# Attention inside a fused block on one core: two running-sum buffers, three low-query buffers, maxima dealt one step earlier, and two more steps per unit summed by GpSimd

## The reference

```
h      = layernorm(x) * (1 + ca) + sa
c_kv   = h @ W_kv_down
k, v   = c_kv @ W_k_up, c_kv @ W_v_up        # 16 heads of 32
q      = h @ W_q
scores = (q k^T + q_rope k_rope^T) / sqrt(64)   # q_rope, k_rope shared by all heads
w      = softmax(causal(scores))
x      = x + ga * ((w v) @ W_o)
h      = layernorm(x) * (1 + cb) + sb
x      = x + gb * (sigmoid(xr W_r^T) * (relu(xk W_k^T)^2 W_v^T))   # xr, xk: token-shifted mixes of h
```

## Time and profile before

| | |
|---|---|
| median of 3 runs | 3613.83 us (3613.76 to 3614.35) |
| the profiled execution's own time | 3614.24 us |
| its span, first to last instruction | 3612.5 us |
| PE, DVE, ACT, POOL busy over the span | 97%, 71%, 50%, 74% |
| attention stage | 472.6 to 2841.7 us |
| unit 8, from its first score matmul to the next unit's | 1667.66 to 1813.99 us, 146.33 us |
| mean granted TensorE clock | 0.992 |

### The profile page before, as it was taken

One profiled execution on the slowest core, in us unless ns is written; L12 is line 12 of the kernel. 1 busy time (PEld: TensorE's weight loads), 2 busy tenths in 40 slices (PEclk: granted clock), 3 DMA queues, 4 the chain that ended last, 5 costly groups with the idle time before them and its releaser, 6 DMA issues. The chain is left out here.

```text
span 3612.5 us, 54216 instructions
## 1 busy us (share of the span) xinstructions
PE 3494.5 (97%) x19552; PEld 2416.0 (67%) x19552; DVE 2562.3 (71%) x5329; ACT 1820.9 (50%) x3455; POOL 2673.0 (74%) x1194
## 2 busy tenths in 40 slices
PE   8999989999999999999999999999999699999999
PEld 4777756666666666666666666666665488888887
DVE  6676677777777777777777777777775366666665
ACT  2333335555555555565555555555555344444443
POOL 2333349889898898898988989889889566666665
PEclk9999999999999999999999999999999899999999
DMA  5778773463534635536346354463551111212120
GB/s 203 272 271 306 254 175 76 104 145 74 134 86 108 138 82 115 120 92 138 83 100 149 76 124 98 97 141 79 114 132 60 62 59 70 70 70 71 70 70 36
DMA packets 232756, 426.58 MB, mean 118 GB/s; under 512 B 25380, under 2 KB 26916, under 8 KB 232488
## 3 DMA queue, kind: packets, MB, share of 16 engines
q1 hardware_dynamic: 232424, 423.10, 43.5%
q10 hardware_dynamic: 64, 0.02, 0.0%
HBM read 300.86 MB, written 121.65 MB: 117 GB/s over the span
## 5 line engine op out<-in xcount | busy, mean ns | idle before, releaser
L1035 ACT ACTIVATE att_probs<-att_ps_s 128x512 f32<-128x512 f32 (+3 forms) x2560 | 1309.3, 536 | 914.6 <-PE att_ps_s L1195 810.6
L1134 POOL TENSOR_TENSOR att_sum_g<-att_sum_g,att_probs 128x2048 f32<-128x2048 f32 (+3 forms) x400 | 1625.2, 4063 | 46.4 <-ACT att_probs L1035 1.7
L1071 DVE TENSOR_REDUCE att_piece_max<-att_ps_m 128x1 f32<-128x512 f32 x1520 | 963.3, 684 | 303.4 <-PE att_ps_m L1178 300.8
L1194 PE MATMUL att_ps_s<-att_q_a,att_k_a 128*128 128x512 f32 (+3 forms) x2560 | 952.3, 376 | 18.8 <-DMA att_q_b<-att_neg_max 9.0
L1195 PE MATMUL att_ps_s<-att_q_b,att_k_b 65*128 65x512 f32 (+3 forms) x2560 | 932.5, 368 | 0.0
L1074 DVE CUSTOM_DVE_ANT_0 att_ps_m<-att_ps_m,mask_qk 128x128 f32<-128x128 f32 x1008 | 477.7, 513 | 259.7 <-PE att_ps_m L1178 246.2
L1178 PE MATMUL att_ps_m<-att_k_a,att_q_a 128*128 128x512 f32 (+3 forms) x1808 | 643.6, 381 | 1.5 <-DVE att_piece_max L1071 0.9
L1194 PEld LDWEIGHTS att_ps_s<-att_q_a,att_k_a 128*128 128x128 f32 x2560 | 485.7, 190 | 158.3 <-issue 54.0
L1201 PE MATMUL att_ps_o<-att_probs,att_v 128*32 128x512 f32 (+3 forms) x5120 | 547.1, 536 | 4.2 <-POOL att_probs L1115 4.2
L1195 PEld LDWEIGHTS att_ps_s<-att_q_b,att_k_b 65*128 65x128 f32 x2560 | 484.5, 189 | 62.6
L1178 PEld LDWEIGHTS att_ps_m<-att_k_a,att_q_a 128*128 128x128 f32 x1808 | 336.6, 190 | 218.2 <-issue 116.1
(11 more groups left out here) (189 smaller groups left out, 4951.5 us busy)
## 6 DMA issues: line engine op xcount, KB each, us to landing
att_q_a<-s_q_hi SPq DMA_DIRECT2D x128, 256.0 KB, 6.0
att_q_a<-s_qr_hi SPq DMA_DIRECT2D x128, 256.0 KB, 6.6
prj_x_sb<-in_x_dram SPq DMA_DIRECT2D x16, 1024.0 KB, 5.2
s_q_hi<-prj_q_hi SPq DMA_DIRECT2D x16, 1024.0 KB, 4.2
s_q_lo<-prj_q_lo SPq DMA_DIRECT2D x16, 1024.0 KB, 6.0
s_k_hi<-prj_k_hi SPq DMA_DIRECT2D x16, 1024.0 KB, 4.4
s_k_lo<-prj_k_lo SPq DMA_DIRECT2D x16, 1024.0 KB, 6.4
s_v<-prj_v_sb SPq DMA_DIRECT2D x16, 1024.0 KB, 9.1
```

What stands on the lines that cost most here:

```text
L1035: act.activation(probs[t % RING][:, hh, c0:CH], ps_s[(GH * t + hh) % SBANKS][:, c0:CH], ACT.Exp, scale=SCALE).then_inc(probs_ready, 1)
L1071: dve.tensor_reduce(top, ps_m[:, bank, :], AX_X, ALU.max).then_inc(piece_taken, 1)
L1134: pool.tensor_tensor(sum_g[:, :, c0:CH], sum_g[:, :, c0:CH], new, ALU.add).then_inc(sum_added, 1)
L1194: mm(out[:, c0:CH], k_a[:, hh, i * P:(i + 1) * P], q_a[j][:, hh, c0:CH], start=True, stop=False)
```

## The change

It has four parts, all in attention:

1. `SHARE_OF`: step 20 (chunk 2, key block 8) and step 36 (chunk 3, key block 12), both 512 wide, go from T to G.
2. `sum_g` becomes two buffers, `sums[j % 2]`. The first addition of a chunk now waits for the close of the chunk before last.
3. `q_b` has 3 buffers in place of 4, used in turn over all chunks (`low_queries`); the last chunk of the last unit uses buffer 1. SP's loads of low queries are put later accordingly.
4. From unit 1 on each maximum piece is dealt to one step earlier (`plan[t - 1 if u else t]`). `deal` is unchanged, but the shares follow `SHARE_OF` through `streams`.

```diff
+QB_RING = 3
-SHARE_OF = ("GGTT", "GGGGGGGG", "GGGGGGGGTGGT", "GGGGGGTGGGGGTGGT")
+SHARE_OF = ("GGTT", "GGGGGGGG", "GGGGGGGGGGGT", "GGGGGGTGGGGGGGGT")
...
-                plan[t] += some
+                plan[t - 1 if u else t] += some
...
+def low_queries(u, j):
+    return 1 if (u, j) == (NU - 1, TCH - 1) else (TCH * u + j) % QB_RING
...
+        sums = [sb("sum_g0", [P, GH, CH], F32)]
-        sum_g = sb("sum_g", [P, GH, CH], F32)
+        sums += [sb("sum_g1", [P, GH, CH], F32)]
...
-                    load_q(u + 1, 0)
+                    load_q_a(u + 1, 0)
+                    load_q_b(u, 3)
...
-                    load_q(u + 1, 1)
+                    load_q_a(u + 1, 1)
+                    load_q_b(u + 1, 0)
...
-                    load_q(u + 1, 2)
+                    load_q_a(u + 1, 2)
+                    load_q_b(u + 1, 1)
...
-                    load_q(u + 1, TCH - 1)
+                    load_q_a(u + 1, TCH - 1)
+                    load_q_b(u + 1, 2)
...
             def add(u, j, i, mine):
                 s = FIRST[j] + i
+                sum_g = sums[j % 2]
...
-                    pool.wait_ge(closed, TCH * u + j + 1)
+                    pool.wait_ge(closed, max(1, TCH * u + j))
...
-                last = over_keys(ps_d, ones, sum_g, start=opens, stop=not ENDS_ON_PE[j])
+                last = over_keys(ps_d, ones, sums[j % 2], start=opens, stop=not ENDS_ON_PE[j])
```

More of the change, by code:

```diff
@@ L812, in load_q_b @@
         for row, src in ((0, heads["q_lo"][i]), (HD, rotary("qr_lo", i))):
-            sp.dma_start(as_f32(ops["q_b"][j][row:row + HD, :, :]), src).then_inc(ops["qb_in"][j], 16)
+            sp.dma_start(as_f32(ops["q_b"][low_queries(u, j)][row:row + HD, :, :]), src).then_inc(ops["qb_in"][j], 16)
     def load_k_a(u, j):
@@ L842, in attention @@
         ops["q_a"].append(sb("q_a3", [P, GH, CH], F32R))
-        ops["q_b"] += [sb(f"q_b{j}", [2 * HD + 1, GH, CH], F32R) for j in range(1, TCH)]
+        ops["q_b"] += [sb(f"q_b{j}", [2 * HD + 1, GH, CH], F32R) for j in range(1, QB_RING)]
         q_a, q_b = ops["q_a"], ops["q_b"]
+        sums = [sb("sum_g0", [P, GH, CH], F32)]
         probs = [sb(f"probs{i}", [P, GH, CH], F32) for i in range(RING)]
         k_next = ops["k_next"]
-        sum_g = sb("sum_g", [P, GH, CH], F32)
+        sums += [sb("sum_g1", [P, GH, CH], F32)]
         piece_max, row_max, neg_max = (ops[n] for n in ("piece_max", "row_max", "neg_max"))
@@ L924, in _ @@
             load_q_a, load_q_b, load_k_a, load_k_b, load_v, (heads, rotary) = operand_loads(sp, scratch, ops, k_b, kb_in)
-            def load_q(u, j):
-                load_q_a(u, j)
-                load_q_b(u, j)
             def load_k_next(u):
@@ L937, in place_max @@
                 wait_alone(sp, piece_taken, turned(u, j), sp_mark)
-                sp.dma_start(as_f32(q_b[j][2 * HD:2 * HD + 1, :, :]).rearrange("o h (r t) -> o (h r) t", t=P),
+                sp.dma_start(as_f32(q_b[low_queries(u, j)][2 * HD:2 * HD + 1, :, :]).rearrange("o h (r t) -> o (h r) t", t=P),
                              as_f32(neg_max[:, j, :])).then_inc(m_in[j], 16)
@@ L971, in body @@
                     wait_alone(sp, scores_ready, GH * (NSTEP * u + FIRST[1] + STEPS[1]), sp_mark)
-                    load_q(u + 1, 1)
-                else:
+                    load_q_a(u + 1, 1)
+                    load_q_b(u + 1, 0)
+                else:
+                    wait_alone(sp, scores_ready, GH * (NSTEP * u + FIRST[1] + STEPS[1]), sp_mark)
+                    load_q_b(u, 3)
                     load_for_last_stage(1)
@@ L1005, in _ @@
             for j in range(2, TCH):
-                load_q(0, j)
+                load_q_a(0, j)
+                if j < QB_RING:
+                    load_q_b(0, j)
                 load_k_b(0, j)
@@ L1018, in place_first_max @@
                 act.wait_ge(piece_taken, turned(0, j))
-                act.dma_start(as_f32(q_b[j][2 * HD:2 * HD + 1, :, :]).rearrange("o h (r t) -> o (h r) t", t=P),
+                act.dma_start(as_f32(q_b[low_queries(0, j)][2 * HD:2 * HD + 1, :, :]).rearrange("o h (r t) -> o (h r) t", t=P),
                               as_f32(neg_max[:, j, :])).then_inc(m_in[j], 16)
@@ L1194, in scores @@
                 mm(out[:, c0:CH], k_a[:, hh, i * P:(i + 1) * P], q_a[j][:, hh, c0:CH], start=True, stop=False)
-                last = mm(out[:, c0:CH], k_b[:, hh, i * P:(i + 1) * P], q_b[j][0:2 * HD + 1, hh, c0:CH], start=False, stop=True)
+                last = mm(out[:, c0:CH], k_b[:, hh, i * P:(i + 1) * P], q_b[low_queries(u, j)][0:2 * HD + 1, hh, c0:CH], start=False, stop=True)
                 last.then_inc(scores_ready, 1)
```

## The result

| | before | after |
|---|---|---|
| median | 3613.83 us | 3738.31 us (3732.26 to 3740.84) |
| the profiled execution's own time | 3614.24 us | 3736.46 us |
| attention stage | 472.6 to 2841.7 us | 472.3 to 2963.4 us |
| unit 8 | 146.33 us | 153.70 us |
| mean granted TensorE clock | 0.992 | 0.975 |

The ratio is 1.0342 [1.0329, 1.0355]: slower by 124.5 us, where +82 (3696 us, at most 3720) was forecast. The sign was right and the size too small. Of the 122.2 us between the two profiled executions all but about 0.2 lies in attention.

What follows compares the result with a forecast made beforehand. Bound: a loop changing hands between PE, ACT and POOL, POOL last in chunk 2. Per period +2.6 and maxima +2.4 make +5.0; 15 periods +75, unit 0 +4.7, last unit +2.65: +82, 3696 us; eight-in-ten range 3645 to 3720.

Steps and rivals of the forecast that it cites:

- step 20 in leg d: One more POOL addition before the close of chunk 2 lengthens that stretch from 13.43 to 17.2 us, +3.77.
- leg d: POOL's stretch from the exponentials of step 21 to the close of chunk 2, 13.43 us before, 17.2 forecast.
- leg a without maxima: Close of chunk 2 to next unit's addition behind step 6: 80.01 less 0.86 and 0.3, so 78.85 us.
- leg a: PE's stretch from the close of chunk 2 to the next unit's POOL addition behind step 6, 80.01 us before.
- maxima in leg c: PE waits for DVE's earlier maxima behind the close of chunk 1, counted as 0.8 us per unit.
- leg c: PE and ACT's stretch from the close of chunk 1 to the exponentials of step 21, 29.06 us before.
- maxima in leg a: PE waits for DVE's earlier maxima at two places, steps 28 and 4, counted as 0.8 us each.
- the loop: One period of work passing between POOL, PE and ACT, 146.31 us from unit to unit, said to bound the kernel.
- no change: Rival, 5%: the added 2.6 us is given back as earlier turning lets PE through at step 24 and elsewhere; 3614 us.
- faster: Rival, 7%: PE is the bound and POOL finds room at the close of chunk 2; 3548 us in full.
- some 0.2 to 1.2 us of room are left: At the close of chunk 3 POOL still ends early despite step 36's addition; no wait, 0.86 us gained.
- the worse case: Rival, 7%: the close of chunk 3 is late too, another 1 to 2 us per unit, about 3720 us.

Runs made afterwards that it cites:

- e5: The changed kernel with maxima dealt as before and PE given extra products, results overwritten, during its wait at the close of chunk 2: 3651.4 us.
- e1: The changed kernel with PE given five rounds of extra products, results overwritten, during its wait at the close of chunk 2: 3714.6 us.
- e8: The kernel before with two sums, three low-query buffers and only step 20 moved to POOL, maxima dealt as before: 3700.1 us.
- e3: The kernel before with only two sums and three low-query buffers; shares and maxima as before: 3596.1 us.
- e7: The kernel before with two sums, three low-query buffers and only step 36 moved to POOL, maxima dealt as before: 3580.3 us.
- e6: The kernel before with only the new share table; one sum, four low-query buffers, maxima dealt as before: 3700.1 us.
- e2: The changed kernel with the maxima dealt as before, not a step earlier: 3680.4 us.
- e9: As e7, but step 11, the 128-wide last step of chunk 1, goes back to PE: 3574.3 us.
- e4: The kernel before with two sums, three low-query buffers and maxima dealt a step earlier; shares as before: 3613.4 us.
- e10: The kernel before with only the maxima dealt a step earlier: 3636.0 us.

## Why the prediction was wrong

Per period, each term of the sum and what stands in its place:

| step of the prediction | forecast | measured |
|---|---|---|
| step 20 in leg d | +3.77, to 17.2 | +3.87, to 17.28 |
| leg a without maxima | 78.85 | 78.14 (e5) |
| maxima in leg c | +0.8 | +0.78 (e1 less e5) |
| maxima in leg a | +1.6 | +3.20 (e1 less e5) |
| clock behind the wait at close 2 | not in the sum | +1.32 (after less e1) |
| period | 151.3 | 153.62 |

Three rows make nearly all of the miss: the clock +1.32, the maxima in leg a +1.6, leg a without maxima -0.7. Over 15 periods the miss is 35 us. Cut at the closes of chunk 2, attention grew by 4.9 us up to that of unit 0 (4.7 forecast), by 112.7 from there to that of unit 15 (75 forecast) and by 4.3 behind it (2.65 forecast). Together this is the gap from +82 to +122.

*Right: the loop and step 20.* The bound is POOL in leg d, one addition costs 4.70 us there, and what PE saves is worth nothing. e8 puts the loss from the shares on this step; e3 and e7 have gains without it. PE's waits came to 101.7 us in all, as "some 100 us or more" said, but the number is partly luck: at step 25 PE waits 4.7 us a unit and not 5.7 (75 us, not "almost all"), and the rest is at closes 1 and 3. The rivals "no change" and "faster" fall with it. The head start of two sums is not a rival of this: it is what brings leg d from 18.1 (e6) to 17.3.

*Failed: "Step 36 ... some 0.2 to 1.2 us of room are left (more where maxima slow PE), so I count no wait there".* Without the shift this just holds: in e2 and e5 PE does not wait at close 3, and 0.1 us is left. The words in brackets are what failed. The room was worked out from the end of POOL's chain, as if maxima that slow PE left POOL where it was. But POOL starts from PE's work too: in after it has nothing to add at step 30, has caught up, and waits for the exponentials of steps 31 and 32 (1.05 and 1.47 us). From its addition of step 32 the chain to the close is fixed, and the runs give it: 31.8 to 31.9 us (e1, e2, e5, e7, e9, after). In after, 32.23 + 0.08 + 31.79 = 64.10 against 64.11. In e7, 28.69 + 0.39 + 31.81 = 60.89 against 60.88 measured, and PE waits 0.21 us for it. The shift makes the exponentials late and then shortens PE's work behind them (from 33.27 to 32.24 us up to the close, e3 and e4), so it takes room away and gives none. With the shift PE waits 0.8 to 0.9 us at close 3 (after, e1), 16 times, and a delay between close 2 and step 32 goes straight into the period. "Waits at step 1 of a unit would mean the worse case", the prediction said, and they came. That rival had 7% and named the clearings as its cause; the place was right and the cause was not, since the added addition made the chain from step 32 to POOL's last addition 4.15 us longer (27.59 before, 31.74 in after), less than its own 4.70.

*Failed in size: the maxima, 2.4 us a period where 4.0 came.* The mechanism was right: waits of PE's weight loads for DVE went from 73.4 us (70.3 and 3.1, the two rows) to 136.3, and leg c came as worked out (+0.78). In leg a it was 1.6 against 3.20: 2.10 up to close 3, and 1.09 from there to its end. About 1.0 us of the 2.10 is the time that PE gets back in e4 and that POOL's lateness at close 3 keeps from it here. The other part is not explained by any run. In the kernels in which POOL has room the shift cost 1.0 a period (e4 less e3, e10 less before), below my 2.4; so the 2.4 was not the price of the shift in either kernel, and leg c's agreement may be luck, since e4 has 0.06 there.

*Missing: the clock.* The prediction worked out a wait of 5.7 us at close 2 and called it free, since PE had nothing else to do. But behind it PE runs at its lower clock level, 1.32 us lost in each period. The earlier trace rows shows 1.00 over a unit whose close waits are 1.26 and 1.11 us, and I had neither a term nor a rival for a longer one. One row did show it: the earlier trace rows has a close behind a wait of 2.77 us, and its eight matmuls take 1.57 us and not 1.06. The window of before over it:

```profile
2838.85:2840.42 1.57, 1.57 (x12) 0.58 (x16) 0.00 (x0) 0.00 (x0) 0.00 (x0) 0.64 0.00 0
```

The prediction used that row for its wait alone. (In the last unit PE has other rests as well, so it does not say which wait is long enough.) The Trainium skill has this cost on the page "TensorE: Matmul & The Clock Gate" (section "HAM oscillation — how this bites in real kernels"): where PE waits for operands again and again (transfers, on that page), it pays for the fallen clock at every wait and not once. The trace of after agrees: one such fall at each of the 16 closes of chunk 2, 6.8 us long and once 10.2, and the loss of time goes in most units when PE is given products to make meanwhile (e1, e5).

The clock's loss also reaches close 3 whole: it comes ahead of step 32, and POOL passes it on (close 2 to close 3 is 1.37 longer in after than in e1).

*Open.* Leg a without maxima was 0.7 us shorter than worked out (e5), and step 36 alone gained 1.2 us a period (e7 less e3), more than the 0.86 of its ones product; that the planner deals other shares to maxima then may be it, but no run separates this. With the new shares the second sum is worth 20 us (e2 against e6), of which leg d's 0.85 a period makes 13; the rest isn't placed. And the last unit of e7 and of e9 takes 154 us to the end of attention where e3's takes 146; POOL's additions set the end there, as in the earlier trace rows (PE waits 5.5 us at the close of chunk 3, 2.7 in e3), and no run gave that unit a table of its own.

## What to carry to other kernels

Room is a property of a place, not of an engine: where an engine catches up with its input, its lead over the others is gone, and what counts from there is the fixed chain from that input to whoever waits for it. Work that one engine does in 0.86 us and another in 4.70 goes over only where the second is early at the very close that follows (step 36, not step 20), and one table entry per place can be run apart from the rest. A wait of some 5 us on the matrix engine in a busy stretch is not free: price it twice, as the wait and as the slower work behind it. And a size found for one tuning step in one kernel (17 us for the shift) need not be its size in another (58 us): measure it in the kernel that it is meant for.

## What the runs showed of the hardware

In unit 8 of after, a halt of 4.7 us on PE, in a stretch with the granted clock at 1.00 on both sides, had the clock at 0.58 already within the halt and at 0.60 for the 3.6 us behind it; close and values took 1.5 us longer than in the window of before. Products whose result is thrown away, 40 matmuls in 4.5 us, kept it at 1.00 in 12 of the 16 halts of e1 and in all 16 of e5 (where it fell once in attention, before the halt of unit 8); in the other four the clock fell near their start, and they took 5.5 to 6.2 us. In the medians they cost nothing else that the legs show: b, c and d are within 0.03 us of the same kernel without them (e1 and after, e5 and e2), although POOL and ACT were at work beside them.
